# Attention with 64-wide heads: scores from three float16 products, and the first addition of the probabilities on GpSimd

## What is computed

```python
q, k, v = x @ Wq.T, x @ Wk.T, x @ Wv.T          # split into 16 heads of 64
q = q / max(norm(q), 1e-12) * q_scale
k = k / max(norm(k), 1e-12) * k_scale
attn = softmax((q @ k.T) * 64 ** -0.5)
out = (attn @ v) @ Wo.T + bo
```

## Time and profile before

| | us |
|---|---|
| median of 3 runs | 5605.33 (5605.23 to 5605.4) |
| span of the profiled execution | 5817.8 |
| busy in the span: PE, DVE | 4867.1, 3629.7 |
| busy in the span: ACT, POOL | 3333.5, 1360.1 |

### The profile page before, as it was taken

How to read it: one execution, slowest core, us unless ns; L and a number is a source line. 1 busy time by engine, 2 the same in 40 slices (tenths; PEclk the granted TensorE clock), 3 DMA queues, 4 the chain that set the end, 5 groups by cost and what they waited for, 6 DMA issues and landing times. The chain is left out here.

```text
span 5817.8 us, 93955 instructions
## 1 busy us (share of the span) xinstructions
PE 4867.1 (84%) x29648; PEld 2462.7 (42%) x29648; DVE 3629.7 (62%) x7303; ACT 3333.5 (57%) x5317; POOL 1360.1 (23%) x1406
## 2 busy tenths in 40 slices
PE   6999768559989967868888659799999999999578
PEld 2222268524444436842222246344344344344255
DVE  5344453477777775347777761576776776776750
ACT  6999644425555544447888722555665665655422
POOL 1111045424334405532323045000000000000055
PEclk8999879869999988989999876899999999999777
DMA  3222121213333312132323232200000000000222
GB/s 83 65 65 63 42 56 39 62 57 91 87 94 91 88 49 60 40 92 51 66 50 66 56 67 43 48 1 0 0 0 0 0 0 0 0 0 0 70 43 40
DMA packets 228016, 265.41 MB, mean 46 GB/s; under 512 B 36874, under 2 KB 194410, under 8 KB 221352
## 3 DMA queue, kind: packets, MB, share of 16 engines
q1 hardware_dynamic: 184180, 194.46, 12.6%
q0 software_dynamic: 43520, 66.97, 6.4%
HBM read 163.86 MB, written 96.65 MB: 45 GB/s over the span
## 5 line engine op out<-in xcount | busy, mean ns | idle before, releaser
L3968 ACT ACTIVATE prob_wide<-slot_wide 128x1024 f32<-128x1024 f32 x512 | 497.2, 1026 | 181.9 <-PE slot_wide L3856 181.9
L2184 ACT ACTIVATE prob_decay<-slot_decay 128x640 f32<-128x640 f32 x512 | 358.8, 705 | 343.8 <-PE slot_decay L2031 342.5
L1000 ACT ACTIVATE prob_rms<-slot_rms 128x1024 f32<-128x1024 f32 x512 | 503.9, 1090 | 56.5 <-PE slot_rms L834 54.0
L2518 DVE TENSOR_TENSOR slot_decay<-slot_decay,dtab_decay 128x512 f32<-128x512 f32 (+3 forms) x1024 | 454.1, 494 | 130.0 <-PE slot_decay L2010 109.9
L1000 ACT ACTIVATE prob_relative<-slot_relative 128x1024 f32<-128x1024 f32 x512 | 497.8, 1049 | 42.1 <-PE slot_relative L834 40.6
L3856 PE MATMUL slot_wide<-qT_wide,kT_wide 64*128 64x512 f32 x2048 | 509.5, 616 | 8.0 <-ACT prob_wide L3968 8.0
L3300 POOL DMA_INDIRECT xg_choice_b<-xn_rows_choice_b,ids_choice_b x64 | 61.1, 955 | 1910.1 <-DVE ids_choice_b L3570 1891.5
L3870 PE MATMUL obank_wide<-prob_wide,v_wide 128*64 128x512 f32 x2048 | 467.7, 598 | 15.3 <-issue 11.6
L1373 DVE TENSOR_TENSOR prob_relative<-prob_relative,rtab_relative 128x1024 f32<-128x1024 f32 (+1 forms) x256 | 394.9, 1548 | 134.9 <-ACT prob_relative L1000 126.7
L3944 ACT ACTIVATE rinv_wide<-rbank_wide 128x512 f32<-128x512 f32 x128 | 76.4, 597 | 481.2 <-PE rbank_wide L3881 481.2
L4038 DVE TENSOR_TENSOR sums_wide<-sums_wide,prob_wide 128x1024 f32<-128x1024 f32 x256 | 312.8, 1222 | 15.0
(11 more groups left out here) (861 smaller groups left out, 10385.7 us busy)
## 6 DMA issues: line engine op xcount, KB each, us to landing
scratch_decay<-parts_decay SPq DMA_DIRECT2D x192, 128.0 KB, 2.4
qst_decay<-scratch_decay SPq DMA_DIRECT2D x128, 128.0 KB
scratch_rms<-parts_rms SPq DMA_DIRECT2D x96, 128.0 KB
kst_rms<-scratch_rms POOLq DMA_DIRECT2D x96, 128.0 KB, 5.5
kst_decay<-scratch_decay SPq DMA_DIRECT2D x192, 64.0 KB
kin_decay<-scratch_decay SPq DMA_DIRECT2D x192, 64.0 KB
scratch_relative<-parts_relative SPq DMA_DIRECT2D x96, 128.0 KB
kst_relative<-scratch_relative POOLq DMA_DIRECT2D x96, 128.0 KB, 6.2
```

Of the source, the lines that this page charges most:

```text
L1000: nc.scalar.activation(prob[:, Q % 2, p:G:2, at:at + m], slot[:, u % 3].rearrange("p (k c) -> p k c", k=2)[:, :, 0:m], ACT.Exp).then_inc(e ...
L2184: nc.scalar.activation(prob[:, Q % 2, j, 0:c1 - c0], slot[:, u % 3, c0:c1], ACT.Exp).then_inc(exp_done, 1)
L2518: last = nc.vector.tensor_tensor(sl, sl, dtab[:, h, 0:m], ALU.mult)
L3968: nc.scalar.activation(prob[:, Q % 2, u % 4, :], slot[:, u % 2, :], ACT.Exp).then_inc(exp_done, 1)
```

## The change

Scores. `qT` and `kT` become float16 with two parts each, a high part (index 0) and the rest (index 1). ScalarE writes the high part of the queries (times 2**14) and of the keys (times a weight); VectorE then makes the low parts: the scaled bank minus the high part, rounded to float16. Only the low parts free the banks of `bench`. S is six float16 products for each unit, three for each head, added up in PSUM: low keys by high queries, high keys by low queries, high by high. The exponential divides the scale out again, with a scale per partition (`peak[:, 1:2]`) where it had none. That scale is made once, at the start of the stage, from the largest product of the two learned scales: two more loads and seven small or 128x1024 instructions on VectorE.

Sum. The first of the three additions moves from VectorE to GpSimd; VectorE's second waits for it (`half_summed`).

```diff
-        kT = sb("kT", [P, C, S])
-        qT = sb("qT", [P, C, S])
+        kT = sb("kT", [P, 2, C, S], F16)
+        qT = sb("qT", [P, 2, C, S], F16)
...
-                        for hh in range(2):
-                            r = slice(W * hh, W * hh + W)
-                            last = nc.tensor.matmul(slot[:, u % 2, hh * S:(hh + 1) * S], kT[r, Q, kb * P:(kb + 1) * P],
-                                                    qT[r, Q, :], start=True, stop=True)
+                        for i, (kp, qp) in enumerate(PRODUCTS):
+                            for hh in range(2):
+                                r = slice(W * hh, W * hh + W)
+                                last = nc.tensor.matmul(
+                                    slot[:, u % 2, hh * S:(hh + 1) * S], kT[r, kp, Q, kb * P:(kb + 1) * P],
+                                    qT[r, qp, Q, :], start=(i == 0), stop=(i == len(PRODUCTS) - 1),
+                                    skip_group_check=True)
...
+                        act.wait_ge(turn_filled, m * (2 * C) + (2 * c + 1))
+                        nc.scalar.activation(qT[:, 0, c, :], bench[:, 0, :], ACT.Copy, scale=HALF_MAX
+                                             ).then_inc(q_high, 1)
                         act.wait_ge(turn_filled, m * (2 * C) + (2 * c + 2))
-                        nc.scalar.activation(kT[:, c, :], bench[:, 1, :], ACT.Copy, scale=kw[:, c:c + 1]
-                                             ).then_inc(k_turned, 1)
+                        nc.scalar.activation(kT[:, 0, c, :], bench[:, 1, :], ACT.Copy, scale=kw[:, c:c + 1]
+                                             ).then_inc(k_high, 1)
...
-                        nc.scalar.activation(prob[:, Q % 2, u % 4, :], slot[:, u % 2, :], ACT.Exp).then_inc(exp_done, 1)
+                        nc.scalar.activation(prob[:, Q % 2, u % 4, :], slot[:, u % 2, :], ACT.Exp, scale=peak[:, 1:2]
+                                             ).then_inc(exp_done, 1)
...
+                    if step == "SUM" and a[1] == 0:
+                        Q = a[0]
+                        pool.wait_ge(exp_done, b * UNITS + (4 * Q + 2))
+                        nc.gpsimd.tensor_tensor(sums[:, Q % 2, :], prob[:, Q % 2, 0, :], prob[:, Q % 2, 1, :], ALU.add
+                                                ).then_inc(half_summed, 1)
...
-                        dve.wait_ge(turn_filled, m * (2 * C) + (2 * c + 1))
-                        nc.vector.tensor_copy(qT[:, c, :], bench[:, 0, :]).then_inc(q_turned, 1)
+                        dve.wait_ge(q_high, m * C + (c + 1))
+                        nc.vector.scalar_tensor_tensor(out=qT[:, 1, c, :], in0=bench[:, 0, :], scalar=HALF_MAX,
+                                                       in1=qT[:, 0, c, :], op0=ALU.mult, op1=ALU.subtract
+                                                       ).then_inc(q_turned, 1)
+                        dve.wait_ge(k_high, m * C + (c + 1))
+                        nc.vector.scalar_tensor_tensor(out=kT[:, 1, c, :], in0=bench[:, 1, :], scalar=kw[:, c:c + 1],
+                                                       in1=kT[:, 0, c, :], op0=ALU.mult, op1=ALU.subtract
+                                                       ).then_inc(k_turned, 1)
                     if step == "SUM":
...
+                        if i == 1:
+                            dve.wait_ge(half_summed, b * C + (Q + 1))
+                        if i:
+                            add = nc.vector.tensor_tensor(sums[:, Q % 2, :], sums[:, Q % 2, :], prob[:, Q % 2, i + 1, :],
+                                                          ALU.add)
```

More of the change, by code:

```diff
@@ L3584, in wide_attention @@
     FIRST_TURNS = 2
+    HALF_MAX = 2.0 ** 14
+    PRODUCTS = ((1, 0), (0, 1), (0, 0))
     ctx = ExitStack()
@@ L3634, in wide_attention @@
         raw = prob[:].rearrange("p a b c -> p (a b c)")
+        all_scales = [sums[:, i] for i in range(2)]
         QR = 3 * C * D
@@ L3640, in wide_attention @@
                  (scales[:, 0, :], A[w["qs"]].rearrange("(c a) o d -> c (a o d)", a=2)),
-                 (scales[:, 1, :], A[w["ks"]].rearrange("(c a) o d -> c (a o d)", a=2)), (bo_t[:], rows(A[w["bo"]]))]
+                 (scales[:, 1, :], A[w["ks"]].rearrange("(c a) o d -> c (a o d)", a=2)), (bo_t[:], rows(A[w["bo"]])),
+                 (all_scales[0], rows(A[w["qs"]].rearrange("h o d -> (h o d)"))),
+                 (all_scales[1], rows(A[w["ks"]].rearrange("h o d -> (h o d)")))]
         HALVES_AT = {(1, "C"): (0, 0), (2, "A"): (0, 1), (2, "B"): (1, 0), (2, "C"): (1, 1), (3, "A"): (2, 0),
@@ L3928, in do @@
                         act.wait_ge(setup_pe, C + 1)
-                        nc.scalar.copy(kw[:], obank[:, 0:C]).then_inc(setup_act, 1)
+                        act.wait_ge(setup_dve, 2)
+                        nc.scalar.activation(kw[:], obank[:, 0:C], ACT.Copy, scale=kinv[:, 0:1]).then_inc(setup_act, 1)
                         act.wait_ge(setup_act, C + 1)
@@ L3973, in _, with do @@
                 nc.scalar.preload_act_table_set("exp_and_others")
+            @block.gpsimd
+            def _(pool):
+                def do(b, step, *a):
+                    if step == "SUM" and a[1] == 0:
[3 more added lines that the diff above has]
+                                                ).then_inc(half_summed, 1)
+                walk(pool, do)
             @block.vector
@@ L4036, in do @@
                         dve.wait_ge(exp_done, b * UNITS + (4 * Q + i + 2))
-                        first = prob[:, Q % 2, 0, :] if i == 0 else sums[:, Q % 2, :]
-                        add = nc.vector.tensor_tensor(sums[:, Q % 2, :], first, prob[:, Q % 2, i + 1, :], ALU.add)
-                        if i < 2:
+                        if i == 1:
[3 more added lines that the diff above has]
+                                                          ALU.add)
+                        if i == 1:
                             link(add)
-                        else:
+                        if i == 2:
                             add.then_inc(summed, 1)
```

14 lines of the change are left out of this document (13 added, 1 removed).

## The result

The changed kernel takes 5715.12 us (median of 4 runs, 5712.02 to 5717.7), the kernel before 5605.28 beside it: a ratio of 1.0199, with a 95% interval of 1.0185 to 1.0214. It is slower by 110 us. The forecast was 5660, and its range ended at 5694.

A forecast was written before the change was run, and what follows sets the result against it. TensorE was taken to bound the stage, with VectorE nearly the second bound in quads 2 to 4. 5605.3 + 50 (15 periods at +3.3) + 5 (edges) = 5660 us; range for 8 in 10, 5574 to 5694.

The forecast's parts named there:

- Prices: Instruction costs: two-unit S saves 0.50 to 0.54 us, exponential 0 to +0.1, turn parts about 0.69, GpSimd's addition 1.9 to 2.3.
- What the engines do to each other: VectorE's two-SBUF-input instructions and GpSimd's each wait for the other's whole instruction, in order of asking; one-SBUF-input reductions are not held.
- Quads 1 to 4: Stretch to the end of R of quad 4, 50.55 us before: +1.5 at a hold of 2.3, 0.0 at 1.9.
- Late or first: Whether GpSimd asks after or before quads 5 to 7's second sum ends: period +0.8 to +2.3 late, +3.2 to +6.1 first.
- +3.3: Added us per period, taken as the middle of the late and first cases; over 15 periods, +50 us.
- The clock: TensorE's granted clock in the stage was expected to stay at 1.00, as in the period with 1.43 us of idle.
- signs of being wrong: Sums and NORM unstretched beside GpSimd, R of quad 4 starting 3 us earlier, or a granted clock below 1.00.
- Edges: Outside the periods: six turns in a row +4 us, setup +4 at most, block 15 -2, block 0's S -1; together +5.
- the chains cost more: Case with GpSimd first everywhere and a hold of 2.3, +6.1 us a period: 5702; within the slower-through-ports chance of 0.60.
- The scores are no cheaper: Rival: float16 at the old price, S stays at 1.99 us, up to +4 a period on the forecast, 5720; chance 0.02.
- Hidden: Rival: GpSimd's addition costs VectorE nothing, -2.6 us a period, 5571 in all; chance 0.24 for faster.
- cancels: Rival: a hold below 1.9 or one beside a reduction, GpSimd late; 0 to +0.8 us a period, 5605 to 5617; chance 0.14.

The follow-up runs named there:

- The experiment with GpSimd late: The changed kernel, with GpSimd also waiting for the third sum of the quad before its addition: 5637.8 us, ratio 1.0061.
- filling: The changed kernel with superfluous TensorE products during its waits, four ahead of R of quad 4 and two ahead of quad 7's: 5687.83 us, ratio 1.0153.

## Why the prediction was wrong

The direction and the mechanism were right; the size was half, 55 us of 110. By its own steps:

- **Prices.** S 1.47 (1.45 to 1.49 forecast), the exponential +0.10 (up to +0.1), GpSimd's addition 2.36 to 2.39 where nothing holds it up (1.9 to 2.3: just above the upper bound), the turn's parts 0.69 and 0.74 (0.69). None of these is off by as much as 0.1.
- **What the engines do to each other.** Right, and shown: an addition that nobody needs costs 111 us; the addition that is needed costs about 130 over the kernel without it in one instruction and about 75 in four; and the reductions are not held.
- **Quads 1 to 4.** +1.68 for a forecast of 0.0 to +1.5. Without the addition R of quad 4 ends 3.19 earlier (3.4 forecast), and the three holds sum to 4.29 us (4.9 at 2.3). One of the three fell on NORM of quad 4 where I had put it on the sums, for the same price. The 0.9 us by which R is longer was not foreseen.
- **Late or first: the first step that failed.** I took +3.3, a middle over two questions, the hold (1.9 or 2.3) and the order (late or first), since the margin was small. The hold came out just above 2.3, which left +2.3 and +6.1, and GpSimd was first in quads 5, 6 and 7 of all 14 periods. My own best numbers had said so: exponentials that end at 7.65 us behind R, and a second sum that ends at 7.9. Measured in quad 5 of the rows above: GpSimd asks at 4331.24, 7.72 behind the end of R, and the sum ends at 4331.33, 7.81. What GpSimd has to be ahead of is the start of the third sum, a little later still. It is ahead by 0.21 there, by only 0.07 in quad 5 of most periods, and by 0.52 and 0.40 in quads 6 and 7. So the margin was small, and its sign was in the working. A choice of this kind has no middle: the same order came out in every period, so +3.3 was a value that no case gave at the hold that was measured. The experiment with GpSimd late gave it the other sign and 77 us back.
- **The clock: the second step that failed.** I expected 1.00, since a wait of 1.43 us had left it there, and named less than that among my signs of being wrong. The waits grew to 3.87 and 2.29 us, and in 14 periods the clock fell during or right behind each of the first kind and behind all but two of the second. It cost 1.53 us a period. My working had the wait of R of quad 4 in it and did not ask what lay beyond 1.43.
- **Edges.** The six turns in a row cost 6.9 us (21.5 for 14.6 from the first turn to V; 4 forecast). A part of that is the clock: it is 0.50 from 3538.8 to 3546 us and 0.53 from 3552.9 to 3560.3, where the kernel before has 1.00 from its third turn on. How much is not shown. The setup cost 2.0 (up to 4), the last block -1.2 (-3 with the first quads). Together that is 7.7 for 5.

The account of the 55 us that were missing: "first" without dips is 113.88 - 108.42 = 5.46 a period, 2.16 over the 3.3 that I took, 32 us in 15 periods; the dips 1.53, or 23 us; the edges 3. Together 58, near enough. The case that I called "the chains cost more" (5702) had what happened, without the dips. "The scores are no cheaper" (5720) lies nearer in its number, but by chance, since S did fall to 1.47. "Hidden" and "cancels" are out.

## What to carry to other kernels

Count what GpSimd does to VectorE instruction by instruction: an addition that frees VectorE of 1.2 us held it here for up to 2.04, and what it holds may be a tiny product on the path. When a forecast hangs on which of two engines asks first, give it the sign that the best numbers give and price both signs as cases, not the middle; and if the order is bad, one wait more can set it. When a wait of TensorE grows past those that the trace shows at full clock, price R and what follows at the lower clock too.

## What the runs showed of the hardware

- Which VectorE instructions are held: beside GpSimd's addition the sums and NORM (two inputs in SBUF), the 128x32 products, and a 128x4 product by constants with one input in SBUF (1.23 us for 0.17). Not held: reductions, the layer norm's statistics, and products with one input in PSUM (0.74 in the middle of an addition). The Trainium skill (SBUF — State Buffer, SBUF: two separate sides) names as users of the shared ports, beside two SBUF inputs, VectorE's two-port modes; the held 128x4 product agrees if it runs in one, which no row here says.
- TensorE's granted clock stayed at 1.00 in the whole loop of the kernel before, through its waits of 1.43 us. With the addition back on VectorE it stayed there behind most waits of 1.74 to 1.83, but fell to its lower level behind four of 14 waits of 1.75 (ahead of a PV) and behind one of 13 of 1.82 (ahead of V); only the last of these made its period longer, 111.93 for 110.30. In the changed kernel it fell at all 14 waits of 3.87 and at 12 of 14 of 2.2 to 2.3: V took 1.98 at 4360.43 and 3.42 a period earlier. With the addition alone moved it fell at 13 of 14 waits of 3.8. That is why the periods of these kernels are uneven.
- Eight records of filling took 3.60 us where R's four take 1.03. The single records of the trace tell why: the filling's, all into one half of the bank, start 0.43 us apart, while R's two products, into different halves, start 0.006 apart (4314.788 and 4314.794). So four products of filling take more than three times as long as R's two.
